# Rotary turn moved from TensorE products to VectorE, and the row position term made with the queries as the stationary operand

## The reference

```python
qkv = (x.reshape(B, L, dim) @ w_qkv + b_qkv).reshape(B, L, 3, nh, hd)
...
def rot(t):
    tr = t.reshape(B, nh, L, hd // 2, 2)
    t0, t1 = (tr[..., 0], tr[..., 1])
    return jnp.stack([t0 * c - t1 * s, t0 * s + t1 * c], axis=-1).reshape(B, nh, L, hd)
q = rot(q)
k = rot(k)
attn = jnp.einsum('bnqd,bnkd->bnqk', q, k) * scale
rel_h = jnp.einsum('bnhwc,hkc->bnhwk', q6, bias_h)
rel_w = jnp.einsum('bnhwc,wkc->bnhwk', q6, bias_w)
attn = attn.reshape(B, nh, H, W, H, W) + rel_h[..., :, None] + rel_w[..., None, :]
attn = jax.nn.softmax(attn.reshape(B, nh, L, L), axis=-1)
out = jnp.einsum('bnqk,bnkd->bnqd', attn, v)
```

## Time and profile before

| | |
|---|---|
| median of 3 runs | 3307.79 us (3305.24 to 3314.67) |
| the profiled execution: time | 3309.41 us |
| its span, first to last instruction | 3307.6 us, so 1.8 us lie around it |
| PE busy | 2748.0 us (83%) |
| DVE busy | 2366.0 us (72%) |
| ACT busy | 1557.4 us (47%) |
| POOL busy | 1335.6 us (40%) |
| mean granted TensorE clock | 0.948 of 2.4 GHz |

### The profile page before, as it was taken

The page is one execution under the profiler, slowest core; times in us unless marked ns, Lnnn a source line. Parts: engine busy times, 40 slices in busy tenths (PEclk is TensorE's granted clock), DMA queues, the critical chain, the costliest instruction groups (busy, mean ns, idle before and its releaser), DMA issues. The chain is left out here.

```text
span 3307.6 us, 40573 instructions
## 1 busy us (share of the span) xinstructions
PE 2748.0 (83%) x15824; PEld 1382.7 (42%) x15824; DVE 2366.0 (72%) x2262; ACT 1557.4 (47%) x1908; POOL 1335.6 (40%) x636
## 2 busy tenths in 40 slices
PE   3577777887678876777667999989998999989999
PEld 1222223332233332222222665556554665555655
DVE  1598899999999999999982466625664356625665
ACT  4445644555435564444431356514563346514564
POOL 4478766887668876766651100011000200011000
PEclk8789998999999999999896999999999999999999
DMA  1334443355443544445541111020111110020110
GB/s 61 128 115 133 153 144 141 130 140 159 145 149 127 140 159 145 161 134 144 182 137 60 30 33 52 1 71 1 33 52 40 33 33 25 29 71 1 33 52 20
DMA packets 93429, 297.51 MB, mean 90 GB/s; under 512 B 15804, under 2 KB 18504, under 8 KB 93224
## 3 DMA queue, kind: packets, MB, share of 16 engines
q1 hardware_dynamic: 93224, 294.73, 28.6%
HBM read 238.57 MB, written 23.07 MB: 79 GB/s over the span
## 5 line engine op out<-in xcount | busy, mean ns | idle before, releaser
L1608 POOL TENSOR_TENSOR arena<-arena 128x1024 f32<-128x1024 f32 x384 | 902.9, 2365 | 325.9 <-DVE arena L1092 277.3
L1092 DVE TENSOR_TENSOR_SCAN arena<-PS,arena 128x1024 f32<-128x1024 f32 x384 | 878.2, 2287 | 86.1 <-ACT PS L1445 62.5
L1445 ACT ACTIVATE PS<-arena,a_inf,a_neg 128x1024 f32<-128x1024 f32 x384 | 463.8, 1208 | 776.8 <-DVE arena L1092 772.4
L564 PE MATMUL PS<-arena,ident 128*128 128x512 f32 x1568 | 804.1, 639 | 19.3 <-ACT arena L1456 15.1
L1225 DVE CUSTOM_DVE_ANT_1 arena<-PS,arena 128x1024 f32<-128x1024 f32 x384 | 467.6, 1219 | 350.4 <-PE PS L851 350.4
L1533 ACT ACTIVATE arena<-arena,neg_max 128x1024 f32<-128x1024 f32 x384 | 441.0, 1149 | 513.4 <-DVE neg_max L1225 513.4
L555 PE MATMUL PS<-arena,sel 96*128 96x512 bf16 x768 | 247.7, 406 | 413.0 <-DVE arena L1100 409.3
L1100 DVE TENSOR_TENSOR arena<-arena,PS 128x1024 f32<-128x1024 f32 x384 | 459.3, 1196 | 9.7 <-PE PS L555 8.9
L564 PEld LDWEIGHTS PS<-arena,ident 128*128 128x128 f32 x1568 | 318.5, 204 | 304.2 <-issue 246.9
L851 PE MATMUL PS<-arena 64*128 64x512 f32 x1536 | 433.1, 641 | 11.1 <-DMA arena<-arena 11.1
L862 PE MATMUL PS<-ident,arena 128*128 128x128 f32 x3072 | 413.9, 278 | 2.6 <-ACT arena L1533 2.6
(11 more groups left out here) (125 smaller groups left out, 2286.2 us busy)
## 6 DMA issues: line engine op xcount, KB each, us to landing
arena<-b_rows SPq DMA_DIRECT2D x256, 512.0 KB, 3.7
arena<-b_rows SPq DMA_DIRECT2D x256, 256.0 KB, 4.0
arena<-arena SPq DMA_DIRECT2D x192, 128.0 KB, 2.9
arena<-arena SPq DMA_DIRECT2D x120, 64.0 KB, 2.0
normed<-xn SPq DMA_DIRECT2D x5, 1536.0 KB, 6.4
normed<-x_in SPq DMA_DIRECT2D x4, 1536.0 KB, 7.9
residual<-x_in SPq DMA_DIRECT2D x4, 1536.0 KB, 8.0
x<-residual SPq DMA_DIRECT2D x4, 1536.0 KB, 6.4
```

Of the source, the lines that this page charges most:

```text
L564: last = pe.matmul(dst[:, half(h)], lhs, rhs[:, half(h)], start=start, stop=stop, skip_group_check=True)
L1092: dve.tensor_tensor_scan(HS[:, at % 2, ::step], DA[:, ::step], DBU[:, at % R3, ::step], 0.0, ALU.mult, ALU.add).then_inc(scan_done.sem, 1)
L1445: act.activation(DA, DELTA[:, tile % 2, :], ACT.Exp, bias=a_inf[:, col:col + 1], scale=a_neg[:, col:col + 1]).then_inc(da_ready.sem, 1)
L1608: pool.tensor_tensor(DBU[:, at % R3, :], DU[:, tile % 2, :], BSB[:, at % R3, :], ALU.mult).then_inc(dbu_ready.sem, 1)
```

## The change

1. The rows of w_qkv's q and k parts are ordered on the host so that the first channels of all pairs of a group lie on partitions 0 to 63 and the second ones on 64 to 127. The turn jobs and their matrix go; DVE makes the sine products from RAW itself, two instructions of 64 partitions that read one half and write the other. The sign is in the table. These stand 4 steps behind their proj job, the other jobs' DVE part 2 steps, as before.
2. A head's rotated q is then in two pieces of 16 rows, so q and k take 8 DMAs a head in place of 4, with rel 10 in place of 6; the bytes are the same. SP issues them in the same places.
3. The roles of the axes are swapped: the column term goes into QX (one-hot of the key's column), and the row term is added by biased_scores, with a broadcast along the innermost axis. It is made with 32 queries as the stationary operand and the table as the moving one (relh jobs), and comes out with queries on the partitions, so nothing is transposed. rel jobs go from 4 + 8 to 2 + 4; relw jobs (2 + 4, of 4 transposes) become relh jobs (2 + 4, of 16 products of 128x32 by 128 columns).
4. JOBS[1] has 14 jobs in place of 24, JOBS[2] 2 in place of 4, at new steps; START puts two value blocks into each rel job and the last two behind the relh jobs.

The core of the diff:

```diff
-HEAD_DMAS = 6
+HEAD_DMAS = 10
+HALF_HEAD = HD // 2
...
-        START = [(m, ()) for m in range(5)] + [(5, (0,)), (6, ()), (7, (1,)), (8, (2,)), (9, (3,)), (10, (4,)),
-                                               (11, (5,)), (None, (6, 7)), (12, ()), (13, ())]
-
-        JOB_AT = [{2 + m * 6 // 5: m for m in range(len(JOBS[1]))}, {6 + 4 * m: m for m in range(len(JOBS[2]))}, {}]
+        JOBS = [[("proj", n) for n in range(4)] + [("rel", 0), ("rel", 1), ("relh", 0), ("relh", 1)],
+                [("proj", n) for n in range(4, 10)] + [("rel", n) for n in range(2, 6)]
+                + [("relh", n) for n in range(2, 6)],
+                [("proj", 10), ("proj", 11)]]
+        START = [(m, ()) for m in range(4)] + [(None, (0, 1)), (4, (2, 3)), (5, (4, 5)), (6, ()), (7, ()),
+                                               (None, (6, 7))]
+        JOB_AT = [{k: m for m, k in enumerate([2, 4, 6, 8, 10, 12, 16, 18, 20, 22, 24, 25, 26, 27])}, {6: 0, 10: 1}, {}]
...
-                    rows = slice(HD * j, HD * j + HD)
-                    q, k = QKC[rows, PLACE[g, "q"], :], QKC[rows, PLACE[g, "k"], :]
-                    rel = RELC[j::HG, g // 2, 0, :]
-                    return [(QX[0:HD, j, :], q), (QX[2 * HD:3 * HD, j, :], q),
-                            (KX[0:HD, j, :], k[:, 0:HALF]), (KX[2 * HD:3 * HD, j, :], k[:, HALF:L]),
-                            (QX[HD:2 * HD, j, :], rel), (QX[3 * HD:4 * HD, j, :], rel)]
+                    copies = [[], [], [(QX[2 * HD * h + HD:2 * HD * h + 2 * HD, j, :], RELC[j::HG, g // 2, :])
+                                       for h in range(2)]]
+                    for h in range(2):
+                        for odd in range(2):
+                            at = XT * odd + HALF_HEAD * j
+                            rows = slice(2 * HD * h + HALF_HEAD * odd, 2 * HD * h + HALF_HEAD * (odd + 1))
+                            copies[0].append((QX[rows, j, :], QKC[at:at + HALF_HEAD, PLACE[g, "q"], :]))
+                            copies[1].append((KX[rows, j, :], QKC[at:at + HALF_HEAD, PLACE[g, "k"], half(h)]))
+                    return copies
...
-                    elif kind == "turn":
-                        pe.wait_ge(raw_saved.sem, raw_saved.after(b, n + 1))
-                        pe.matmul(dst, W["turn"][:, 0, :], RAW[n if n < 4 else n % 2], start=True, stop=True
-                                  ).then_inc(turn_psum.sem, 1)
-                    elif kind == "relw":
+                    elif kind == "relh":
                         g, h = divmod(n, 2)
-                        pe.wait_ge(rel_saved.sem, rel_saved.after(b, 12 if g else 4))
-                        for t in range(QB // 2):
-                            at = h * HALF + t * P
-                            last = pe.transpose(dst[:, t * P:(t + 1) * P], RELC[:, g // 2, 1, at:at + P], idn)
-                        last.then_inc(relw_psum.sem, 1)
+                        pe.wait_ge(rope_ready.sem, rope_ready.after(b, (2, 6, 8)[g]))
+                        for r in range(IMG // 2):
+                            at = h * IMG // 2 + r
+                            t, row = divmod(r, HG)
+                            last = pe.matmul(dst[IMG * row:IMG * row + IMG, t * P:(t + 1) * P],
+                                             QKC[:, PLACE[g, "q"], at * IMG:(at + 1) * IMG],
+                                             W["rel_h"][:, 0, HG * (IMG - 1 - at):HG * (REL - at)],
+                                             start=True, stop=True, skip_group_check=True)
+                        last.then_inc(relh_psum.sem, 1)
...
-                        dve.tensor_tensor(RT2[:, h, :], src, W["sin"][:, 0, half(h)], ALU.mult
+                        dve.tensor_tensor(RT2[0:XT, h, :], raw[XT:P, :], W["sin"][XT:P, 0, half(h)], ALU.mult)
+                        dve.tensor_tensor(RT2[XT:P, h, :], raw[0:XT, :], W["sin"][0:XT, 0, half(h)], ALU.mult
                                           ).then_inc(sin_done.sem, 1)
...
-                        in1=bias.rearrange("p (o w) -> p o w", o=1).to_broadcast([P, IMG, IMG]),
+                        in1=bias.rearrange("p (h o) -> p h o", o=1).to_broadcast([P, IMG, IMG]),
```

More of the change, by code:

```diff
@@ L348, in build @@
         PLACE = {(0, "q"): 0, (0, "k"): 1, (1, "q"): 0, (2, "q"): 2, (1, "k"): 1, (2, "k"): 1}
[L349 to L354, removed]
-        START = [(m, ()) for m in range(5)] + [(5, (0,)), (6, ()), (7, (1,)), (8, (2,)), (9, (3,)), (10, (4,)),
-                                               (11, (5,)), (None, (6, 7)), (12, ()), (13, ())]
-        JOB_AT = [{2 + m * 6 // 5: m for m in range(len(JOBS[1]))}, {6 + 4 * m: m for m in range(len(JOBS[2]))}, {}]
-        ROPE_FOR, REL_FOR = [4, 10, 12], [4, 12, 12]
+        JOBS = [[("proj", n) for n in range(4)] + [("rel", 0), ("rel", 1), ("relh", 0), ("relh", 1)],
[5 more added lines that the diff above has]
+        JOB_AT = [{k: m for m, k in enumerate([2, 4, 6, 8, 10, 12, 16, 18, 20, 22, 24, 25, 26, 27])}, {6: 0, 10: 1}, {}]
+        ROPE_FOR, REL_FOR = [4, 10, 12], [2, 6, 6]
         def job_bank(phase, m):
@@ L513, in _ @@
                     for j in range(HG):
-                        for dst, src in operands(0, j)[2 * k:2 * k + 2]:
+                        for dst, src in operands(0, j)[k]:
                             sp.dma_start(dst, src).then_inc(head_loaded[j].sem, 16)
@@ L521, in _ @@
                         sp.wait_ge(s_psum.sem, s_psum.after(b, STEPS * g - HG + j + 1))
-                        for dst, src in operands(g, j):
+                        for dst, src in itertools.chain(*operands(g, j)):
                             sp.dma_start(dst, src).then_inc(head_loaded[j].sem, 16)
@@ L786, in value_product @@
                         last.then_inc(v_psum.sem, 1)
-                job_saved = {"proj": raw_saved, "turn": sin_done, "rel": rel_saved, "relw": relw_saved}
+                job_saved = {"proj": raw_saved, "rel": rel_saved, "relh": relh_saved}
                 def job(phase, m, blocks=()):
@@ L1166, in job @@
                         last.then_inc(rel_saved.sem, 1)
-                    elif kind == "relw":
+                    elif kind == "relh":
                         g, h = divmod(n, 2)
-                        dve.wait_ge(relw_psum.sem, relw_psum.after(b, n + 1))
-                        dve.tensor_copy(RELW[g][:, half(h)].rearrange("p (t j k) -> p t j k", j=HG, k=IMG),
+                        dve.wait_ge(relh_psum.sem, relh_psum.after(b, n + 1))
+                        dve.tensor_copy(RELH[g][:, half(h)].rearrange("p (t j k) -> p t j k", j=HG, k=IMG),
                                         src.rearrange("p (t k j) -> p t j k", j=HG, k=IMG)
-                                        ).then_inc(relw_saved.sem, 1)
+                                        ).then_inc(relh_saved.sem, 1)
                 def save_turned(s):
@@ L1238, in _ @@
                     biased_scores(s)
-                    if k - 2 in JOB_AT[g]:
-                        job(g + 1, JOB_AT[g][k - 2])
+                    for after, kinds in ((4, ("proj",)), (2, ("rel", "relh"))):
+                        if k - after in JOB_AT[g] and JOBS[g + 1][JOB_AT[g][k - after]][0] in kinds:
+                            job(g + 1, JOB_AT[g][k - after])
                     if g + 1 == GROUPS and k - 2 in LATE_AT:
@@ L1705 @@
     mats["w_out"] = wo
-    mats["w_qkv"] = np.asarray(L1_conv_w_qkv)
+    pos = np.arange(P)
+    paired = HD * (pos % XT // HALF_HEAD) + 2 * (pos % HALF_HEAD) + pos // XT
+    qkv_order = np.arange(3 * C)
+    for k in range(2 * GROUPS):
+        qkv_order[k * P:(k + 1) * P] = k * P + paired
+    mats["w_qkv"] = np.asarray(L1_conv_w_qkv)[:, qkv_order]
     mats["w_proj"] = np.asarray(L1_conv_w_proj)
@@ L1712 @@
     ang = np.concatenate([(tok % IMG).astype(f)[:, None] * freqs, (tok // IMG).astype(f)[:, None] * freqs], 1)
[L1713 to L1715 removed]
+    mats["cos"] = np.cos(ang).T[pos % HALF_HEAD]
+    mats["sin"] = np.sin(ang).T[pos % HALF_HEAD] * np.where(pos < XT, 1, -1)[:, None]
     mats["ident"] = np.eye(P)
@@ L1718 @@
     mats["to_high"] = np.eye(P, k=XT)
-    turn = np.zeros((P, P), f)
-    for i in range(0, P, 2):
-        turn[i + 1, i] = -1.0
-        turn[i, i + 1] = 1.0
-    mats["turn"] = turn
     mats["chan_mean"] = np.full((P, P), 1.0 / DI)
```

67 lines of the change are left out of this document (27 added, 40 removed).

## The result

| | before | after |
|---|---|---|
| median | 3308.88 us (3305.24 to 3314.67, 5 runs) | 3324.98 us (3323.19 to 3328.87, 5 runs) |
| ratio, 95% interval | | 1.0049 [1.0034, 1.0064] |
| span of the profiled execution | 3307.6 us | 3323.2 us |
| mean granted TensorE clock | 0.948 | 0.932 |

The changed kernel is 0.3 to 0.6% slower, just over what can be told from none. The medians lie 16 us apart where 7 were forecast (3315), and 3325 is inside the likeliest case's range of 3303 to 3329. On another chip, without any edit, the ratio was 1.0031 [1.002, 1.0042].

The account below looks back on a forecast made before the run. PE was taken to bound each image, with SP's issue of head copies level with it at changes of head group. 3309.4 - 85 (PE's work) + 91 (issues and clock) = 3315 us; range over all 3275 to 3332.

Parts of the forecast that it names:

- likeliest case: At each change of head group SP's issue at 0.59 us binds and eats PE's gain: 3315 us, 3303 to 3329; chance 0.68.
- PE's gain, 85 us: Work taken off PE in image start and both group loops: 21.2 us an image, 85 in four.
- (c): Group 1's loop: two turning products on even steps go, 1.8 us gained an image.
- sine pair: DVE's two sine products: +0.6 us, up to 3 with waits for POOL, lying in DVE's gaps, so counted as nothing.
- (a): Start of each image: turning products and two rel jobs go; scores(0) at +38.3, 7.7 us gained (7 to 8.8).
- (b): Group 0's loop, up to the release: six turning products and four rel jobs go, 11.7 us gained an image.
- SP's issue, 8 x 10.35: Each of eight changes of head group: 16 more issues at 0.633 us, 10.1 us, plus 0.25 for long issues.
- The clock, 8 x 1.0: Low PE clock after the last wait at each of eight changes of head group: 1.0 us more each.
- R2: Head-copy issues of 16 rows are cheaper: 3271 us at 0.42 us each, 3291 at 0.5; chance 0.14.
- R3: After each change of head group two stretches at 1.2 GHz, 3.4 us lost instead of 1.4: 3331 us; chance 0.08.
- R4: DVE sets the pace, by a dearer broadcast or sine products blocked by POOL each step: 3400 us or more; chance 0.04.
- R5: relh jobs aren't as fast as weigh(), 2 us a job, 4 us more an image: 3331 us; chance 0.04.

## Why the prediction was right, and by how much it was off

**PE's gain, 85 us.** Right as a sum: 86.6 us less in the kernel with six copies, 21.2 us less between images. Its halves compensate: 48 for the row term where its steps say 42, 38.5 for the rotation where they say 45 (the 85 are 2 us less than these together, as scores(0) was put at +38.3 and not at PE's own +37.8). The stretches of images 2 to 4 show where, for the kernel before, the row term alone, and the whole change with six copies:

| us, mean of images 2 to 4 | before | row term | whole, six copies | gained | forecast |
|---|---|---|---|---|---|
| PE's first product to scores(0) | 46.9 | 40.8 | 38.4 | 8.5 | 7.7 |
| scores(0) to the release for group 1 | 105.7 | 100.0 | 94.0 | 11.7 | 11.7 |
| scores(35) to the release for group 2 | 73.4 | 73.4 | 72.8 | 0.6 | 1.8 |

The steps of group 0's loop came out to a tenth. The start gave more than forecast and group 1's loop a third of it: that the sum came out right to a tenth is luck.

**Group 1's loop, (c), and the sine pair taken at nothing.** Two turning products go, yet only 0.6 us comes out, for in the kernel after PE has a wait there once an image that it didn't have. The chain through it in image 3, and PE's timeline:

```profile
2765.28 0.69 DVE arena L1145
...
2765.98 0.69 DVE arena L1146
...
2766.69 1.23 DVE arena L1175
...
2770.34 0.92 ACT arena L1507
...
2771.30 1.13 PE L852 MATMUL PS<-arena 64*128 64x512 f32 x4 [1.03 <-ACT arena L1507]
```

The two sine products stand right before DVE's copy of turned probabilities and the next biased maximum; behind these come ACT's exponential and copy, and PE waits 1.03 us for the copy. The kernel with six copies has the same wait in each image. The row term's part alone, which keeps one sine product and the turning products, doesn't have it. The forecast put the sine pair at nothing because DVE has idle time on average; in this step it had none to spare.

**Start, (a), in the kernel after.** scores(0) of image 3 was forecast at +38.3 and stands at 2603.78 - 2564.93 = +38.85, so 7.1 us gained where 7.7 were forecast; over images 2 to 4 it is 8.2, as the two others began more slowly in the kernel before. Of POOL and DVE at the start of image 3 after the change the timeline says:

```profile
2571.21 1.77 POOL L1635 TENSOR_TENSOR arena<-arena 128x512 f32<-128x512 f32 x1 [182.91 <-ACT arena L1499]
2573.67 1.26 POOL L1642 TENSOR_TENSOR arena<-arena 128x512 f32<-128x512 f32 x1 [0.69 <-DVE arena L1146]
...
2577.30 1.70 POOL L1642 TENSOR_TENSOR arena<-arena 128x512 f32<-128x512 f32 x1 [0.69 <-DVE arena L1146]
...
2571.17 0.69 DVE L1145 TENSOR_TENSOR arena<-arena 64x512 f32<-64x512 f32 x1 [12.59 <-ACT arena L1499]
2571.87 1.66 DVE L1146 TENSOR_TENSOR arena<-arena 64x512 f32<-64x512 f32 x1
2573.89 1.59 DVE L1145 TENSOR_TENSOR arena<-arena 64x512 f32<-64x512 f32 x1 [0.36 <-ACT arena L1499]
```

A sine product of 64 partitions takes 0.69 us when it starts ahead of POOL's instruction (by 0.04 us in the first row) and 1.6 to 1.66 when it starts behind it, and POOL's takes 1.26 or 1.7 in the same way. From 2571.17 to rope_ready 2 at 2579.00 it is 7.8 us for two half products, 3.9 each: the upper end of the forecast (3.8), where each waits for the other. The Trainium skill, "SBUF — State Buffer", section "Who interferes with whom", says that a DVE instruction with two inputs in SBUF and a GpSimd instruction that reads SBUF shut each other out, and the trace agrees: 2 x 1.26 + 2 x 0.69 = 3.9 is the two one after the other. SP's first copy then goes out at 2579.03, +14.1, later than the upper end of +12.7, since PE's first half products were late too: the granted clock of the first 15 us was 0.81 (0.90 before), and RAW came at +6.2 instead of +5.0. Most of these 1.4 us is taken up before scores(0); heads 1 and 2 of group 0 then come late by 0.47 and 0.62 us, which had been left out. The chain runs through SP's copies here (from 2579.03 to a landing at 2607.09), where it ran through PE: with ten copies a head SP and PE are level at the start of an image too.

**Steps of group 0, (b).** From scores(0) to the release it was 2706.95 - 2601.20 = 105.75 us and is 2698.47 - 2603.78 = 94.7: 11.1 gained, 11.7 forecast. The 0.6 is the late heads: scores(3) starts 5.44 us behind scores(0) where it started 4.76, as the 1.09 us of waits stand in place of one of 0.65 for ACT. Behind it nothing is lost.

**SP's issue, 8 x 10.35.** Right in its mechanism and nearly so in size: 9.8 us at this change (28.6 less 18.8), 9.7 in the mean of the eight, and 0.59 us an issue in all three forms of copy. That bytes and rows don't show in the cost was read from the earlier trace rows and holds. The sign "the two waits before it 3 to 4 us each" holds for head 1 only (2.5 to 4.0 us); head 2's wait is 0.5 to 3.2, shorter where the low clock stretches the work ahead of it.

**The clock, 8 x 1.0: the term that was mis-sized.** It was taken as 1.4 us at each change, 0.4 of it there before, from "at most of them" and one low stretch of 1.7 us. It was there behind the last wait of all eight changes and cost 1.6 to 3.1 us, 2.0 in the mean; filling PE's waits gave back 2.1 a change. So 1.6 to 1.7 more than the 0.4 before, not 1.0: +5 to 6 us in all. (In the second profile of the kernel before it is 1.1 in place of the 0.4, so the excess itself is known to some 0.6 us a change.) The low clock inside the waits was rightly called free.

**The sum over one image**, means of images 2 to 4: 8.2 + 11.1 + 0.6 = 19.9 gained (forecast 21.2), 19.5 lost to issues and 3.5 to the clock, 23.0 (forecast 20.7 and 2.0, 22.7), so +3.1; by the starts of the images it is 376.9 - 374.2 = +2.7 (forecast 2 x 11.35 - 21.2 = +1.5). Too much for the issues and too little for the clock nearly cancel, which is luck again; the mechanism of each was right. Four images make 11 to 12 us, and from the load of residual on the profiles differ by 9.8 and 11.2 us. The medians say 16 and 9.5; what lies above 10 or 12 goes with the scan stage, which differs from profile to profile by up to 7 us for no cause that I found. A forecast of +7 us from two terms of 85 and 91 could as well have come out on the other side of zero.

**The rivals.** R2 (cheap issues of 16 rows) is out by 0.59 us. R3 came in in part: the price per change is 2.1 us, between the 1.4 of the forecast and its 3.4, with 6.1 us of low clock behind two of the eight last waits and 3.2 to 3.6 behind the others. R4 and R5 are out: L1221 at 1,219 ns, and a product of L815 at 273 ns like one of weigh(); of R4 there is only the one wait an image behind the sine pair.

**Left open**: why the low clock takes 1.7 us behind one wait and 3.0 behind another, and what moves the scan stage's end.

## What to carry to other kernels

Count the issues on the queue that feeds the critical path before making transfers smaller: here each cost 0.63 us whatever it moved, so a layout that frees 21 us of the busiest engine per image and cuts six copies into ten was no gain, and with four of the ten dealt to an idle engine's queue it was worth 2.6%. Measure the halves of a change by themselves: the row term alone was worth 1.4% and needed no copy more. When a queue is relieved, look at what stands next in it, for it will now start earlier beside what is still waited for. Where the busiest engine must wait in several short pieces, price the clock behind the last of them, or give it work to do in them. And idle time on average doesn't make a term free: look at the one step where the longer instruction lands.

## What the runs showed of the hardware that was not expected

- A DMA issue on GpSimd's queue took 0.48 us (16 copies of 32 KB in 7.70 us; 24 in 11.50 us, 8 of them of 64 KB), less than SP's 0.59 + 0.04 for the same kind of copy.
- With 16 issues on SP's queue beside 24 on GpSimd's, copies took 5.2 to 6.1 us to land (change to group 2) where they took 2.0 to 3.0 from SP's queue alone, with the DMA engines over 90% busy; with 24 beside 16 they took 2.7 to 3.1. The queues add up only until the engines are full, and these small copies fill them at 160 to 220 GB/s, where the 1,536 KB load moved 417.
- Three products before each wait, which nobody reads, made the kernel 17 us faster.
- A DVE product of 64x512 took 0.69 us, or up to 1.66 when POOL's instruction had started first, and POOL's 128x512 went from 1.26 to 1.7 when DVE's had: whichever starts second waits.
